# Graph network kernel: sort destinations and first windows loaded by two queues, weight transposes in banks of four at another place

## The reference

```
h = relu(layernorm(x))
h = h @ W_enc.T + b_enc
for l in range(2):
    m = relu(concat(h[src], h[dst]) @ msg_W1[l].T + msg_b1[l]) @ msg_W2[l].T + msg_b2[l]
    upd = concat(h, segment_sum(m, dst)) @ upd_W[l].T + upd_b[l]
    h = layer_norm(h + upd, ln_g[l], ln_b[l])
x = x + h @ W_out.T + b_out
h = relu(layernorm(x))
for i in range(3):
    agg = segment_sum(h[src], dst) / degree
    h = agg @ Wl[i].T + bl[i] + h @ Wr[i].T        (relu after the first two)
x = x + h
```

## Time and profile before

| what | value |
|---|---|
| median of 3 runs | 3429.53 us (3422.79 to 3432.8) |
| the profiled execution | 3434.72 us |
| its span from first to last instruction | 3433.0 us |
| PE busy | 2955.7 us (86%) |
| DVE busy | 2576.5 us (75%) |
| ACT busy | 2069.9 us (60%) |
| POOL busy | 619.9 us (18%) |
| mean granted TensorE clock | 0.93 |

### The profile page before, as it was taken

How to read it: one execution, slowest core, us unless ns; L and a number is a source line. 1 busy time by engine, 2 the same in 40 slices (tenths; PEclk the granted TensorE clock), 3 DMA queues, 4 the chain that set the end, 5 groups by cost and what they waited for, 6 DMA issues and landing times.

```text
span 3433.0 us, 220197 instructions
## 1 busy us (share of the span) xinstructions
PE 2955.7 (86%) x88775; PEld 2730.1 (80%) x88775; DVE 2576.5 (75%) x5711; ACT 2069.9 (60%) x3898; POOL 619.9 (18%) x914
## 2 busy tenths in 40 slices
PE   3665665599999998799999997798998799999999
PEld 2554544499988887699988886688888799999999
DVE  6899998677767776677766675799999865556555
ACT  1333333577767776777766775677777555555555
POOL 1211113400011116300011116122222300000000
PEclk7777776799999999899999999899999899999999
DMA  3000000566656662466656563255555478877888
GB/s 69 9 6 6 6 6 20 141 184 183 184 162 174 176 176 76 140 184 185 188 162 171 172 173 61 62 168 165 167 166 165 132 230 266 266 232 228 271 258 253
DMA packets 445075, 518.81 MB, mean 151 GB/s; under 512 B 153683, under 2 KB 321013, under 8 KB 444994
## 3 DMA queue, kind: packets, MB, share of 16 engines
q1 hardware_dynamic: 415959, 499.02, 48.6%
q0 software_dynamic: 4000, 8.20, 2.0%
q10 hardware_dynamic: 25035, 10.60, 1.2%
HBM read 408.98 MB, written 108.65 MB: 151 GB/s over the span
## 4 chain that ended last, share of the span: by engine, by line
PE 70%; DVE 12%; issue 8%; SPq 2%; POOL 2%; DMA 2%; ACT 2%; DVEq 0%; ACTq 0%; POOLq 0%
PE psum L1326 19%; PE psum L1551 17%; PE psum L1344 9%; PE psum L1330 9%; PE psum L1538 6%; PE psum L1518 4%; DVE arena L1590 2%; PE psum L691 1%; PE psum L1526 1%; DVE Hf L929 1%; POOL arena L2026 1%; DVE AGGf L974 1%; POOL tabf L2009 1%; DVE Hf L1068 1%; DVE Hf L2113 1%
## 5 line engine op out<-in xcount | busy, mean ns | idle before, releaser
L1326 PE MATMUL psum<-tabf,arena 125*32 125x128 f16 x40256 | 1105.7, 220 | 68.5 <-issue 27.5
L1326 PEld LDWEIGHTS psum<-tabf,arena 125*32 125x32 f16 x40256 | 953.3, 97 | 144.3 <-issue 100.7
L1330 PE MATMUL psum<-arena 96*32 96x128 f16 x20928 | 1045.3, 221 | 9.5 <-issue 9.5
L1377 ACT ACTIVATE arena<-psum 128x512 f32<-128x512 f32 x1300 | 776.4, 597 | 374.4 <-PE psum L1330 352.6
L1330 PEld LDWEIGHTS psum<-arena 96*32 96x32 f16 x20928 | 701.9, 95 | 12.0 <-issue 7.2
L1551 PE MATMUL psum<-tabr,cellr 125*125 125x256 f32 x5000 | 626.6, 285 | 5.6 <-ACT cellr L1473 5.5
L1551 PEld LDWEIGHTS psum<-tabr,cellr 125*125 125x125 f32 x5000 | 609.2, 188 | 6.9 <-issue 6.8
L1344 PE MATMUL psum<-arena 128*32 128x129 f32 x10400 | 566.0, 277 | 0.4 <-issue 0.4
L1473 ACT CAST cellr<-arena 125x630 fp32r<-125x630 f16 x500 | 359.7, 720 | 270.4 <-PE psum L1551 241.0
L1580 ACT CAST arena<-psum 125x500 f16<-125x500 f32 x625 | 360.8, 578 | 154.5 <-PE psum L1518 117.7
L1473 DVE CAST cellr<-arena 125x630 fp32r<-125x630 f16 x500 | 244.0, 488 | 244.3 <-PE psum L1551 240.4
(11 more groups left out here) (313 smaller groups left out, 4405.8 us busy)
## 6 DMA issues: line engine op xcount, KB each, us to landing
arena<-cells_kept SPq DMA_DIRECT2D x500, 315.0 KB
cells_kept<-arena SPq DMA_DIRECT2D x625, 126.0 KB, 1.7
arena<-slots_turned_from SPq DMA_DIRECT2D x152, 384.0 KB
tabf<-slots_turned_from SPq DMA_DIRECT2D x150, 384.0 KB, 3.4
arena<-slots_turned_from SPq DMA_DIRECT2D x50, 512.0 KB
tabf<-slots_turned_from SPq DMA_DIRECT2D x50, 512.0 KB
arena<-slots_turned_to SPq DMA_DIRECT2D x152, 96.0 KB
tabf<-slots_turned_to SPq DMA_DIRECT2D x150, 96.0 KB, 3.9
```

What stands on the lines that cost most here:

```text
L1326: pe.matmul(psCell[b][q:q + GW, g * D:(g + 1) * D], fr, rows, start=g == 0 and p == 0, stop=False, tile_position=(0, q), skip_group_check= ...
L1330: m = pe.matmul(psCell[b][q:q + GW, g * D:(g + 1) * D], toB[part][:, here + q:here + q + GW], cur[:, part, g, :], start=g == 0 and 4 * k + ...
L1377: act.activation(msgs[:, SLOT[pos], :, 0:D], psCell[SLOT[pos]].rearrange("p (c d) -> p c d", d=D), ACT.Relu).then_inc(f_msg, 1)
```

## The change

Four edits, all in the first part of the sort:

1. `dst` is loaded in two pieces: 112 partitions by the SP queue, the other 13 by the ACT queue, as the first instruction of each. DVE waits for both.
2. The windows of pair 0 are asked for by both queues: the four groups of tile 0 by SP, of tile 1 by ACT, each with its own wait for `o_lo`. All later windows stay on SP.
3. The 16 transposes go four to a bank, into banks 0 to 3, with no wait among them. ACT copies four at a time (4 copies of 512 columns instead of 16 of 128).
4. `prepare_weights` moves. On PE it stands behind `overflow(1)`, `turn(0)` and the ranks of pair 2, ahead of `fill` of pair 1, and waits for the copies of those ranks. On ACT it stands behind those copies and `store(0)`, ahead of `keep_slots` of pair 1. On POOL it stays where it was.

```
+        def window(eng, at, u, g):
+            start = eng.value_load(loi[0:1, at], min_val=0, max_val=E - WIN)
+            c = u * COLS + g * RK
+            for n, ends in enumerate((src, dst)):
+                eng.dma_start(win[:, n, c:c + RK], ends[bass.ds(start, WIN)].rearrange("(p t) -> p t", p=128)).then_inc(o_win, 16)
...
             sp.wait_ge(o_lo, 1)
-            windows(lambda g, u: slice(g * (NT + 2) + u, g * (NT + 2) + u + 1))
+            for g in range(RG):
+                window(sp, slice(g * (NT + 2), g * (NT + 2) + 1), 0, g)
...
             fill(1, 1)
-            pe.wait_ge(o_totc, 4)
-            pe.wait_ge(o_rkc, 8)
-            pe.wait_ge(o_S, 2)
-            prepare_weights()
             overflow(1)
             turn(0, True)
             for u in range(2):
                 ranks(4 + u, u)
+            pe.wait_ge(o_totc, 6)
+            pe.wait_ge(o_rkc, 12)
+            prepare_weights()
             for u in range(2):
                 fill(2 + u, u)
...
+            act.dma_start(dstl[WIDE:P], dst.rearrange("(p t) -> p t", p=P)[WIDE:P]).then_inc(o_dst, 16)
+            act.wait_ge(o_lo, 1)
+            for g in range(RG):
+                window(act, slice(g * (NT + 2) + 1, g * (NT + 2) + 2), 1, g)
             for u in range(2):
                 totals(u, u, True)
                 copy_ranks(u, u, True)
...
                 if m:
                     store(0, 0, slice(1, 3), slice(0, 2), None)
+                    prepare_weights()
                 for u in range(2):
                     keep_slots(2 * m + u, u, slice(2 * m + u, 2 * m + u + 1), 1 if m else None)
                 act.wait_ge(s_h, 1)
                 normalise(lambda w: slice(2 * m + w, 2 * m + w + 1))
-                if m == 0:
-                    prepare_weights()
...
-            dve.wait_ge(o_dst, 16)
+            dve.wait_ge(o_dst, 32)
...
-            sp.dma_start(dstl, dst.rearrange("(p t) -> p t", p=P)).then_inc(o_dst, 16)
+            sp.dma_start(dstl[0:WIDE], dst.rearrange("(p t) -> p t", p=P)[0:WIDE]).then_inc(o_dst, 16)
...
                 for w in range(NW):
-                    if w >= 2:
-                        pe.wait_ge(s_wTc, w - 1)
-                    pe.transpose(psT[w % 2][:, 0:D], wnat[:, w, :], ident[:]).then_inc(s_wT, 1)
+                    pe.transpose(bank[w // 4][:, w % 4 * D:w % 4 * D + D], wnat[:, w, :], ident[:]).then_inc(s_wT, 1)
...
-                for w in range(NW):
-                    act.wait_ge(s_wT, w + 1)
-                    act.copy(wT[:, w, :], psT[w % 2][:, 0:D]).then_inc(s_wTc, 1)
+                for w in range(0, NW, 4):
+                    act.wait_ge(s_wT, w + 4)
+                    act.copy(wT[:, w:w + 4, :], bank[w // 4].rearrange("p (w d) -> p w d", d=D)).then_inc(s_wTc, 4)
```

More of the change, by code:

```diff
@@ L610, in windows @@
                     for g in range(RG):
[L611 to L614, removed]
+                        window(sp, at(g, u), u, g)
             sp.wait_ge(o_lo, 1)
-            windows(lambda g, u: slice(g * (NT + 2) + u, g * (NT + 2) + u + 1))
+            for g in range(RG):
+                window(sp, slice(g * (NT + 2), g * (NT + 2) + 1), 0, g)
             for part in range(2):
```

## The result

| | before | change |
|---|---|---|
| median, same chip | 3428.81 us (6 runs, 3422.79 to 3432.8) | 3409.33 us (6 runs) |
| profiled execution | 3434.72 us | 3408.52 us |
| span, clock | 3433.0 us, 0.930 | 3406.3 us, 0.933 |
| end of the sort (its last large reduce) | 591.3 us | 575.3 us |

The ratio is 0.9942, 95% interval 0.9932 to 0.9953: 19.9 us faster (16.1 to 23.3), where 13.6 were forecast. One of the change's six executions took 6186.92 us; the median of 3409.33 still counts it, the ratio does not, and the median of the other five is 3408.56.

A forecast was written before the change was run, and what follows sets the result against it. DVE was taken to set the sort's pace, so its earlier loop entry shortens the whole. 3.88 + 6.14 + 3.6 = 13.6 us off the median 3429.53 gave 3415.9 us, range 3410 to 3424.

The forecast's parts named there:

- A: Destinations in two pieces: DVE's whole wait to read them goes, 3.88 us.
- B: Windows of pair 0 asked for by two queues: DVE reads them 6.14 us earlier.
- queues in turn: Rival at pair 0's windows: requests served one queue at a time, no gain there, sum 7.5 us; chance 0.12.
- a load no faster: Rival at the destinations: more engines do not speed the load, no gain there, sum 9.7 us; chance 0.05.
- a small piece behind x: Rival at the destinations: the 13-row piece lands only after x, at 24.5, losing 11.9 us; chance 0.05.
- C: Weights banked and moved: payload of pair 2 written at 115.0 instead of 118.57, 3.6 us gained.
- I take its 2 us as hidden: At the weights: ACT's store(0), copies and requests, was to run beside the transposes and cost nothing.
- The 1.45 for POOL: At the weights: POOL's two adds delayed once by DVE's work, 1.45 us added to the path.
- the second such wait: At POOL's adds: one wait for each add instead of one in all, making the weights' gain about 1.4 us smaller.
- The first part of the products: On PE at the weights: only the second part, 768 of 1280 columns, was counted, 1.4 us at full clock.
- The clock's rival: Clock at 1.2 GHz in transposes and products: the weights gain only 0.3 us, sum 10.3 us; chance 0.20.
- the range's low end: Fastest time expected for the whole kernel: 3410 us, from 15.6 us of gain and 4 us of scatter.

The follow-up runs named there:

- e10: The kernel before, word for word, compared with itself on another chip; ratio 1.0004.
- e11: The changed kernel once more, against the kernel before, on another chip than the first; ratio 0.9968.
- e1: The kernel before with only the destinations loaded in two pieces; ratio 0.9991.
- e4: The changed kernel with 66 more statistics operations on DVE (12.9 us), taking the front's gain back; ratio 0.9998 to the kernel before.
- e3: The kernel before with only the weights edits, transposes banked and prepare_weights moved; ratio 0.9988.
- e8: The change with 40 of DVE's 50 statistics moved into its wait for pair 0's windows, and pair 1's windows on two queues; ratio 0.9955 to the kernel before.
- e5: The changed kernel as it is, against the kernel before, on a further chip; ratio 0.9959.
- e7: The change with ACT's four transpose copies ahead of store(0) and the products behind both fills of pair 1; ratio 0.9941 to the kernel before.
- e12: e9 with the last 12 of the 50 weight and bias loads asked for by ACT; ratio 0.9948 to the kernel before.
- e9: e7 plus 40 statistics in DVE's first window wait, ACT's table loaded early, two groups of pair 1's windows on ACT; ratio 0.9956 to the kernel before.

## Why the prediction was wrong

**Direction, places and sizes ahead of the loop were right.** A, "the whole wait: 3.88", came as 3.85. B, "6.14 us less", came as 5.92; ACT's requests stand beside SyncE's at 0.33 to 0.40 us, and the rivals of queues in turn, of a load no faster, and of a small piece behind x did not occur. That rule of the Trainium skill (DMA: Bandwidth & Descriptors, section "Issuing engines are not separate DMA queues") was set against the row of 0.38 us for each request. Issue time on a second queue was worth 5.92 us here: that it is "usually small relative to the DMA itself" may stand for one request (0.38 us, against 1.59 from the last request to DVE's read the earlier trace rows), but not for the sum of sixteen in a row.

**C had the right sum of wrong terms, and that is luck.** The forecast 3.6 came as 3.64 on the first chip and 3.97 with e10 and e11, but as 1.7 to 2.6 on the chip of e1 to e4. From the end of the last rank copy to the payload the prediction counted 12.3 us; the trace has 12.66 (92.59 to 105.25). The transposes were taken from a pair of 125-column ones at 0.39, and took 1.94 in all instead of 3.2. "I take its 2 us as hidden" was wrong for `store(0)`, since faster transposes left it in front of the copies; it and the row of copies cost 2.2 where 0.6 was counted. The 1.45 for POOL was not there, and so still less the second such wait that the prediction names beside it. The first part of the products was taken as hidden behind POOL's adds and only the second counted, 1.4: the whole took 4.1 with the clock low and 2.7 without. The clock's rival ("the clock is low at the weights") came true in half, for products and not for transposes, in four of the six executions that had this order (the first, e3, e4, e8; not e5 and e11).

**The step that failed is the range's low end**, "the upper ends, 15.6 us, and 4 us for the scatter of medians", and the central value with it, as far as one comparison tells. The sum was subtracted from one median of three runs as if the rest of the kernel, five sixths of it, took the same time in both ("a microsecond by which DVE enters the loop earlier should be one at the end"). It does not. The front gained 13.3 and 13.7 us in the two pairs of traces, the three comparisons gave 19.9, 13.9 and 10.9. Two of the three comparisons hold 13.6 in their interval, the first (16.1 to 23.3) does not. That the surplus lies in code that the change leaves alone is what the first pair of traces shows (10.7 us behind the sort, and 2.7 more inside the loop); why this code ran faster just then stays open. That the edits cause it wherever they run is excluded by e4 (-3.1 to 4.4 us left) and by e11 (6.8 to 14.6 in all). An effect of the first chip alone is not excluded. How narrowly the range was missed says little either way: the median before moved from 3429.53 to 3428.81 with three more runs, as much as the 0.67 that is missing.

## What to carry to other kernels

- Sum the gain at a mark just behind the edit and compare traces there: the marks of two pairs of traces, each from one chip, gave 13.3 and 13.7 us where the times of the same two kernels gave 10.9 to 19.9. Compare within a chip: the mark at pair 2 of one and the same kernel lay 2.6 and 3.0 us apart between two chips. A range for the time needs the scatter of unchanged stages, taken from several executions of the same kernel and from more than one chip.
- When a step is moved ahead of a producer, list what its partners have in front of it by then. A step counted as hidden behind a slow neighbour comes out as soon as that neighbour is faster, as `store(0)` did.
- Taking a long step apart (transposes now, products behind the fills, e7) gave 4.1 us more from pair 1 to pair 2 than moving it whole.

## What the runs showed of the hardware

- 16 transposes of 128 x 128 floats into four banks without a wait took 1.94 us in every trace of that order, at clock 1.00; before, two banks in turn with a copy between, 6.48 at 0.50.
- The two requests for x together held the SP queue for 19.43 us before (from 1.21; 19.04 of them are the second's), and for 13.13 with the destinations on 112 partitions ahead. No window waited for it in either.
- The requests for pair 0's windows, on both queues at once, stayed at 0.33 to 0.40 us each. SyncE's weight request beside ACT's broadcast rows took 1.12 in e12 and 0.43 in e9, where ACT asked for nothing; which of the things that differ made it longer is not shown.
